# Keeping V of all batches in SBUF, and a first key projection by contraction halves, in a fused attention and mixture-of-experts kernel

## The reference

```python
x = x + tanh(g_xattn) * xattn(layernorm(x), ctx)      # 4 x 512 x 256, 16 heads of 16
x = x + tanh(g_ffn) * ffn(layernorm(x))

def xattn(x, mem):                     # 512 queries and 512 keys in each of 4 batches
    k, v = split(mem @ W_kv); q = x @ W_q
    return softmax(q @ k.T / 4) @ v @ W_proj + b_proj

def ffn(x):                            # 2048 tokens, 8 experts, the best 2 of each token, and a shared one
    logits = x @ gate_w.T; weights = softmax(top2(logits))
    return shared(x) + sum over the 2 chosen e of weight * (silu(x @ wg[e].T) * (x @ wu[e].T)) @ w_down[e].T
```

## Time and profile before

| | |
|---|---|
| median of 3 runs | 529.23 us |
| profiled execution, its own time | 531.15 us |
| its span (first to last instruction) | 529.4 us |
| TensorE busy | 503.8 us, 95% of the span |
| VectorE, ScalarE, GpSimd busy | 56%, 51%, 32% |
| moved by DMA | 58.60 MB |

### The profile page before, as it was taken

The page is one execution under the profiler, slowest core; times in us unless marked ns, Lnnn a source line. Parts: engine busy times, 40 slices in busy tenths (PEclk is TensorE's granted clock), DMA queues, the critical chain, the costliest instruction groups (busy, mean ns, idle before and its releaser), DMA issues.

```text
span 529.4 us, 8545 instructions
## 1 busy us (share of the span) xinstructions
PE 503.8 (95%) x2972; PEld 316.4 (60%) x2972; DVE 295.5 (56%) x537; ACT 271.9 (51%) x436; POOL 171.8 (32%) x193
## 2 busy tenths in 40 slices
PE   8989899999999999999989989999999999999992
PEld 6645423333333333334456456589999999999991
DVE  3665777887887888883565993233333333333321
ACT  1756267777777777775564301205444444444430
POOL 4400166672211111111000003004655666665542
PEclk9999989999999999999999998999999999999997
DMA  7999419987773666300013002112444333344332
GB/s 253 305 284 255 185 36 254 250 200 216 195 178 92 169 170 169 81 1 23 0 41 120 1 0 80 41 41 71 65 66 69 63 61 61 62 66 66 63 45 30
DMA packets 44882, 58.60 MB, mean 111 GB/s; under 512 B 6352, under 2 KB 36688, under 8 KB 44336
## 3 DMA queue, kind: packets, MB, share of 16 engines
q1 hardware_dynamic: 29536, 36.12, 25.7%
q0 software_dynamic: 7488, 10.23, 11.9%
q10 hardware_dynamic: 7824, 11.81, 6.7%
HBM read 37.89 MB, written 20.05 MB: 109 GB/s over the span
## 4 chain that ended last, share of the span: by engine, by line
PE 76%; DVE 9%; DMA 8%; issue 2%; ACT 2%; SPq 2%; POOLq 1%; POOL 0%; DVEq 0%
PE ps L1095 59%; PE ps L1181 12%; DMA out<-unit_region 5%; DMA x_sb<-in_x 2%; PE ps L1189 2%; PE ps L1467 1%; DVE neg_max L819 1%; DMA unit_region<-qk_parts 1%; DVE ctx_region L1022 1%; DVE unit_region L1014 1%; SPq L344 1%; DVE unit_region L931 1%; ACT ctx_region L675 1%; PE ps L1298 1%; DVE stats L776 1%
## 5 line engine op out<-in xcount | busy, mean ns | idle before, releaser
L819 DVE TENSOR_REDUCE neg_max<-ps 128x2 f32<-128x1024 f32 x128 | 151.2, 1219 | 43.3 <-PE ps L1095 42.9
L675 ACT ACTIVATE ctx_region<-ps 128x512 f32<-128x512 f32 x256 | 139.9, 595 | 58.8 <-PE ps L1095 58.6
L1095 PE MATMUL ps<-unit_region 96*128 96x512 bf16 (+1 forms) x512 | 134.1, 383 | 4.5 <-DMA unit_region<-qk_parts 2.1
L1095 PE MATMUL ps<-unit_region,ctx_region 128*128 128x128 f32 (+1 forms) x968 | 115.4, 277 | 2.5 <-DVE x_sb L938 2.5
L1095 PEld LDWEIGHTS ps<-unit_region,ctx_region 128*128 128x128 f32 (+1 forms) x968 | 111.7, 190 | 3.7 <-DVE x_sb L938 3.4
L1095 PEld LDWEIGHTS ps<-unit_region 96*128 96x128 bf16 (+1 forms) x512 | 48.4, 99 | 98.3 <-ACT ctx_region L675 58.9
L562 POOL DMA_INDIRECT out<-unit_region x39 | 61.8, 1585 | 55.7 <-DMA out<-unit_region 50.8
L535 POOL DMA_INDIRECT unit_region<-x_rows,unit_region x39 | 38.6, 989 | 123.0 <-DVE unit_region L1049 81.0
L1095 PE MATMUL ps<-dn_region,unit_region 128*128 (+1 forms) x330 | 78.2, 379 | 0.0
L741 ACT COPY ctx_region<-up_region 128x1536 f32 x39 | 57.3, 1472 | 35.0 <-PE ps L1095 34.9
L1181 PE MATMUL ps<-ctx_region,unit_region 128*32 128x512 f32 x512 | 68.7, 609 | 2.2 <-ACT ctx_region L675 0.7
(11 more groups left out here) (151 smaller groups left out, 407.6 us busy)
## 6 DMA issues: line engine op xcount, KB each, us to landing
up_region<-in_w_upT ACTq DMA_DIRECT2D x9, 768.0 KB, 4.3
qk_parts<-up_region SPq DMA_DIRECT2D x32, 192.0 KB, 3.2
unit_region<-qk_parts SPq DMA_DIRECT2D x32, 192.0 KB, 4.5
v_rows<-dn_region SPq DMA_DIRECT2D x4, 1024.0 KB, 5.9
unit_region<-qk_parts SPq DMA_DIRECT2D x32, 128.0 KB, 4.4
unit_region<-v_rows SPq DMA_DIRECT2D x16, 256.0 KB, 5.5
dn_region<-in_w_downT ACTq DMA_DIRECT2D x9, 384.0 KB, 5.5
ctx_region<-in_ctxT SPq DMA_DIRECT2D x4, 512.0 KB, 10.9
```

Of the source, the lines that this page charges most:

```text
L675: nc.scalar.activation(probs[:, k % 8, :], bank(4 + k % 2), ACT.Exp).then_inc(exp_done, 1)
L819: nc.vector.tensor_reduce(neg_max[:, s, 2 * p:2 * p + 2], bank(2 * (p % 2), 2), AX.X, ALU.max, negate=True).then_inc(max_done, 1)
L1095: return nc.tensor.matmul(o_, w, m, start=start, stop=stop)
```

## The change

V gets a home in SBUF for each batch: batches 0, 1 and 2 in `dn_region` (batch 2 where `resid` was), batch 3 in `unit_region`. `v_rows`, `send_v` and `load_v` go, with 4 stores of 1024 KB and 16 loads of 256 KB. The ones are set in three memsets at the old place, and a fourth once the last `low_part` is through. The w_down loads of ScalarE are moved to slots in which their place in `dn_region` is free. The first key projection waits for each half of the contraction by itself (`first_k`), and for that w_kv's K half and ctx of batch 0 are loaded in two halves each; w_kv's V half goes to ScalarE's queue and x of batch 0 to SP's, behind them. TensorE's loop over slots is written out. Its wait for `whole_sb` is moved from ahead of slot 0 to step 3 of it.

```diff
+PARTS_SENT = {1: (0, 1), 5: (2,), 9: (3,)}
+UP_AT = (1, 2, 3, 5, 6, 7, 9, 10, 11)
+DOWN_AT = (13, 14, 15, 5, 6, 9, 10, 11, 1)
-    v_rows = nc.dram_tensor("v_rows", (B, P, TB, H * VW), F32, kind="Internal").ap()
...
+        V_AT = (2 * DC * T, 2 * DC * T + v_words, 0)
+        def v_home(b):
+            home = (dn_region[:, V_AT[b]:V_AT[b] + v_words] if b < len(V_AT) else unit_region[:, 4 * HG * T:unit_words])
+            return home.rearrange("p (k h w) -> p k h w", k=TB, h=H)
...
-            sp.dma_start(wkv_sb[:, :, 0:D], w_kv_rows[:, :, 0:D]).then_inc(wk_in, 16)
-            load_ctx(0)
-            sp.dma_start(wkv_sb[:, :, D:2 * D], w_kv_rows[:, :, D:2 * D]).then_inc(wv_in, 16)
+            for d in range(DC):
+                sp.dma_start(wkv_sb[:, d, 0:D], w_kv_rows[:, d, 0:D]).then_inc(k_half[d], 16)
+                sp.dma_start(ctx_sb[:, d, 0:T], ctxT[d * P:(d + 1) * P, 0:T]).then_inc(k_half[d], 16)
+            sp.dma_start(x_sb[:, 0:TB, :], x_dram[:, 0:TB, :]).then_inc(x_in[0], 16)
...
             send_k(0)
-            send_v(0)
             send_q(0)
...
-            nc.gpsimd.memset(v_sb[:, :, :, :, HD:VW], 1.0).then_inc(v_ones, 1)
-            pool.wait_ge(v_ones, 1)
+            for n, b in enumerate((0, 1, 3)):
+                nc.gpsimd.memset(v_home(b)[:, :, :, HD:VW], 1.0).then_inc(v_ones, 1)
+                pool.wait_ge(v_ones, n + 1)
...
+            pool.wait_ge(low_done, len(QK_ORDER) // 2)
+            nc.gpsimd.memset(v_home(2)[:, :, :, HD:VW], 1.0).then_inc(v_ones, 1)
...
-            act.dma_start(x_sb[:, 0:TB, :], x_dram[:, 0:TB, :]).then_inc(x_in[0], 16)
+            act.dma_start(wkv_sb[:, :, D:2 * D], ...[:, :, D:2 * D]).then_inc(wv_in, 16)
...
-                if b >= 2:
-                    act.wait_ge(v_out[b - 2], 16)
+                if b == 2:
+                    act.wait_ge(low_done, len(QK_ORDER) // 2)
...
+            for u in range(1, UNITS):
+                if u in PARTS_SENT: (waits for k_out and q_out of these batches, as before)
+                if u in UP_AT:
+                    load_up(UP_AT.index(u))
+                if u in DOWN_AT:
+                    if u > NG:
+                        act.wait_ge(pv_done, (u - 1) // NG * NG * TB)
+                    load_down(DOWN_AT.index(u))
                 exp_slot(u, u % NG, more_max=u + 1 < UNITS)
...
-                    last = nc.tensor.matmul(bank(6)[...], v_unit[:, s, kt, h * VW:(h + 1) * VW],
+                    last = nc.tensor.matmul(bank(6)[...], v_home(u // NG)[:, kt, u % NG * HG + h, :],
...
-                pe.wait_ge(v_in[s], 16 * (bu + r // NG + 1))
+                pe.wait_ge(v_done, u // NG + 1)
...
                         if first:
                             pe.wait_ge(nmT_sb, 1)
+                            pe.wait_ge(whole_sb, len(WHOLE_ORDER))
...
+            def first_k():
+                for d in range(DC):
+                    pe.wait_ge(k_half[d], 16 * 2)
+                    for c in range(DC):
+                        last = mm(bank(K_BANK + c), wkv_sb[:, d, c * P:(c + 1) * P], ctx_sb[:, d, 0:T], d == 0, d == DC - 1)
+                last.then_inc(k_ps, 1)
...
             pe.wait_ge(ones_rows, 1)
+            pe.wait_ge(v_ones, B)
             pe.wait_ge(rowsT_sb, B)
-            pe.wait_ge(whole_sb, len(WHOLE_ORDER))
             slot(0, 0, 0, first=True)
-            with pe.Fori(0, B - 1) as b:
-                for r in range(1, NG + 1):
-                    slot(b * NG + r, b, r)
+            for u in range(1, UNITS - 3):
+                slot(u, (u - 1) // NG, (u - 1) % NG + 1)
```

More of the change, by code:

```diff
@@ L244, in build @@
         ctx_in = [sem(f"ctx_in{b}") for b in range(B)]
-        wk_in, wv_in, wq_in = sem("wk_in"), sem("wv_in"), sem("wq_in")
+        k_half = [sem(f"k_half{d}") for d in range(DC)]
+        wv_in, wq_in = sem("wv_in"), sem("wq_in")
         gates_in = sem("gates_in")
@@ L367, in send_k @@
                 send_parts(1, b, k_out[b])
[L369 to L372, removed]
             def send_q(b):
@@ L391, in _ @@
                 load_rows(0, g, 0, q_unit, Q_RUNS)
[L392 to L395, removed]
             for g in range(2, NG):
@@ L568, in _ @@
         def _(act):
-            act.dma_start(x_sb[:, 0:TB, :], x_dram[:, 0:TB, :]).then_inc(x_in[0], 16)
+            act.dma_start(wkv_sb[:, :, D:2 * D], w_kv.rearrange("(c p) n -> p c n", p=P)[:, :, D:2 * D]).then_inc(wv_in, 16)
             act.dma_start(wq_sb[:, :, :], w_q.rearrange("(c p) n -> p c n", p=P)).then_inc(wq_in, 16)
@@ L613, in copy_v @@
                     act.wait_ge(v_ones, 1)
-                if b >= 2:
-                    act.wait_ge(v_out[b - 2], 16)
-                nc.scalar.copy(v_sb[:, b % 2, :, :, 0:HD],
+                if b == 2:
+                    act.wait_ge(low_done, len(QK_ORDER) // 2)
+                nc.scalar.copy(v_home(b)[:, :, :, 0:HD],
                                bank(V_BANK, 2).rearrange("p a (k h w) -> p (a k) h w", k=2, h=H)).then_inc(v_done, 1)
@@ L650, in _, with load_up, load_down @@
             whole_q(3)
[L652 to L657, removed]
+            def load_up(e):
+                act.dma_start(w_up[:, e, :, :], w_upT[e, :, :].rearrange("(c p) f -> p c f", p=P)).then_inc(w_ffn_in, 16)
+            def load_down(e):
+                act.dma_start(w_dn[:, e, :, :], w_downT[e, :, :].rearrange("(c p) n -> p c n", p=P)).then_inc(w_ffn_in, 16)
             def copy_max(u):
@@ L681, in _ @@
             exp_slot(0, 0, first=True)
-            for b in range(B):
-                act.wait_ge(v_out[b], 16)
-            for b in range(B - 1):
-                for late in ((0, 1), (2,), (3,))[b]:
-                    act.wait_ge(k_out[late], 16 * QK_OUTS)
-                    act.wait_ge(q_out[late], 16 * QK_OUTS)
-                for r in range(1, NG + 1):
-                    if r < NG:
-                        load_expert(b * 3 + r - 1)
-                    exp_slot(b * NG + r, r % NG)
-            for u in range(UNITS - 3, UNITS):
+            for u in range(1, UNITS):
+                if u in PARTS_SENT:
+                    for b in PARTS_SENT[u]:
+                        act.wait_ge(k_out[b], 16 * QK_OUTS)
+                        act.wait_ge(q_out[b], 16 * QK_OUTS)
+                if u in UP_AT:
[4 more added lines that the diff above has]
+                    load_down(DOWN_AT.index(u))
                 exp_slot(u, u % NG, more_max=u + 1 < UNITS)
@@ L1180, in pv @@
                 for h in range(HG):
-                    last = nc.tensor.matmul(bank(6)[h * VW:(h + 1) * VW, :], v_unit[:, s, kt, h * VW:(h + 1) * VW],
+                    last = nc.tensor.matmul(bank(6)[h * VW:(h + 1) * VW, :], v_home(u // NG)[:, kt, u % NG * HG + h, :],
                                             probs[:, (kt * HG + h) % 8, :], start=kt == 0, stop=kt == TB - 1,
@@ L1235, in _ @@
             TURN_MAX, TURN_OUT = 3, 9
-            for b in range(2):
-                project_k(b, 0)
-                project_k(b, 1)
+            def first_k():
[4 more added lines that the diff above has]
+                last.then_inc(k_ps, 1)
+            for b in range(2):
+                if b == 0:
+                    first_k()
+                else:
+                    project_k(b, 0)
+                    project_k(b, 1)
                 project_v(b, (0, 1))
```

18 lines of the change are left out of this document (3 added, 15 removed).

## The result

The changed kernel takes 532.30 us in the median of 9 runs (530.39 to 533.98); the kernel before took 529.55 us beside it (9 runs, 528.89 to 530.81). The ratio is 1.0047, with a 95% interval of 1.0030 to 1.0064: it is slower by 2.75 us. The prediction was 527.9 us in a range of 526.4 to 530.6, with a chance of 0.18 for slower. The profiled execution of the changed kernel took 532.3 us, with a span of 530.5 us.

A forecast was written before the change was run, and what follows sets the result against it. TensorE, busy 95% of the span, was taken to bound the kernel, with a chain of waits in the first 82 us; +1.0 - 0.6 - 1.5 - 0.2 = -1.3 us from 529.23 gave 527.9 us, range 526.4 to 530.6.

The forecast's parts named there:

- the term of +1.0 us: x of batch 0 behind 768 KB lands at 10.2 (bounds 8.8 to 12.2), delaying `first_pair(0, 0)` by 1.0 us (0 to +3.0).
- the clock in the projections: TensorE's clock falling in idleness ahead of `turn_xn(0)` or `first_pair(0, 0)`; left out of the sum, kept as a rival.
- the landing less 9.2: Delay of the chain to `first_pair(0, 0)` equals the landing time of x of batch 0 minus 9.2 us.
- The first key projection, up to 0.43 us sooner: With half the data needed, the projection begins up to 0.43 us sooner; the gain ends at `turn_xn(0)`.
- The slower rival: Clock falls in the projections, first at `turn_xn(0)` after 1.7 us idle (1.3 on the chain); both places 530.9 us; chance 0.15.
- the second place: TensorE's wait ahead of `first_pair(0, 0)`, where a fall of the clock would cost 1.7 us.
- The moved wait and the clock at slot 0, -0.6 and -1.5: At slot 0, less waiting for `whole_sb` gains 0.6 us; the clock staying at 2.4 GHz from 66 to 70 gains 1.5.
- the signs of being wrong: x landing before 9 or after 12, the clock falling at another place, or the slots getting shorter.
- V's traffic at nothing: In the attention slots, taking 8 MB of V's transfers out of the DMA rings gains nothing by itself.
- the loop, -0.2 to -0.3: Writing out TensorE's loop over slots saves 0.2 us at two round ends (bounds 0 and -0.3).
- the w_down loads at nothing: Loads ahead of slots 13 to 15 on ScalarE's queue cost 0, at most +1.4 us; rival +0.2, 529.4 us, chance 0.05 with the rest.
- their cover of 2 us: Memsets start at 14.0 and `copy_v(0)` needs the first at 17.1; without cover 0.9 us goes on the path.

The follow-up runs named there:

- ctx_halves: Changed kernel with K projected in one piece and w_kv's K half loaded whole, ctx of batch 0 still in two halves; 530.86 us, ratio 1.0035 to the kernel before.
- swap_whole: Changed kernel with whole loads and K projected in one piece, x of batch 0 still behind 768 KB on SP's queue; 528.48 us, ratio 0.9992 to before.
- old_start: Changed kernel with the loads and first key projection of the kernel before, rest of the change kept; 527.78 us, ratio 0.9975 to before.
- filler: Changed kernel with 14 transposes of nothing on TensorE ahead of `turn_xn(0)`; 532.34 us, ratio 1.0060 to the kernel before.
- new_start: Kernel before with only the changed kernel's start (halves, w_kv's V half on ScalarE's queue, x on SP's); 534.18 us, ratio 1.0087 to before.
- whole_ahead: Changed kernel with the wait for `whole_sb` back ahead of slot 0; 533.81 us, ratio 1.0078 to the kernel before.
- wait_only: Kernel before with only the wait for `whole_sb` moved to step 3 of slot 0; 528.52 us, ratio 0.9973 to before.

## Why the prediction was wrong

**The step that failed is the landing of x of batch 0, the term of +1.0 us; the runs give +2.8.** A second failed with it, the clock in the projections, which the sum put at nothing and which cost 1.5. The rule of the first, the landing less 9.2, was good: 12.0 gives +2.8 for the changed kernel, and 11.8 gives +2.6 for ctx_halves, where `apply_rows(1)` came 2.4 us later. Its size was off. I had costed x by the bytes ahead of it, between two landings of whole loads. swap_whole shows that this gives 9.7. The halves, which I had only counted as bytes, brought it to 12.0, the upper part of my own bounds.

**The first key projection, up to 0.43 us sooner**: it started at 7.61 instead of 7.70, but its second half landed at 9.5, where the whole ctx of batch 0 had landed at 7.6. It then took 3.93 us instead of 3.67, and V's products started 0.17 us later than before, at 11.38. The halves gained nothing over the kernel before, and they are what separates the changed kernel from swap_whole, 3.8 us; x's place on the queue costs at most the 0.7 us between swap_whole and old_start, whose intervals overlap.

**The slower rival came true at its first place.** `turn_xn(0)` found TensorE idle for 2.58 us, not 1.7, and the clock fell; the transposes and V's second half took 0.7 and 1.0 us longer. The rival's price for this was 1.3; the profiles above give 1.5. I had set against it that 2 us of idleness at 34 to 36 let the clock stand, which was one stretch of one profile. At the second place, ahead of `first_pair(0, 0)`, it stood this time too. Over the profiles it fell behind idle times of 2.6, 2.6, 3.0, 3.2 and 4.5 us and stood behind 1.2, 1.2, 1.4 and (filler) 2.4 us.

**Not foreseen: `high_k(0)` waits too.** ScalarE takes the standard deviation of batch 0, which needs x, ahead of it; it ran at 14.07, though K was ready at 11.5. In the kernel before it ran at 11.4. Behind the same x, VectorE's residue and the parts of K of batch 0 came later. It isn't on the chain here, and no run separates it.

**The moved wait and the clock at slot 0, -0.6 and -1.5.** The wait was right: 0.7 to 0.8 us in the profiles. The clock's term was right in size for the one profile it was read from (1.1 us up to the first product with V and some 0.5 us behind it), but it was taken off a median that need not have had that fall, and new_start and whole_ahead keep the wait and show no fall there. Both steps together are 1.4 us (0.3 to 2.6) by wait_only's ratio and 0.5 by its medians, where the sum had 2.1. How often the clock falls can be read from the mean granted clock over the span of the 111 runs of the kernel before beside the experiments: 0.995 in 17 runs, which average 527.2 us; 0.991 or 0.992 in 67, 529.1 us; 0.988 or 0.989 in 24, 530.9 us. The profiled execution, with 531.15 us, is like the third group, the median like the second. It tells the number of falls and not their place: the profile of before has two stretches of low clock ahead of 500 us, at 66 to 70 and at 316 to 324, the changed kernel's has one at 16 to 20 and one at 320 to 324, and which of the two the median run of before lacks is not known. For the changed kernel 4 of 9 runs have 0.991 (530.9 us) and 5 have 0.988 or less (533.1 us). So part of the 2.75 us is that it goes one level down more often, and 1.8 us is the distance at the level of 0.991.

**The sum with the measured terms**: +2.8 (x) + 1.5 (clock in the projections) - 1.4 (wait and clock at slot 0) - 0.3 (loop) = +2.6 us, against 2.75 measured. The third term is known only to about 1 us, so the agreement is partly luck. Of the signs of being wrong that the prediction named, one came (the clock fell at another place), and one stood at its edge (x after 12).

**Right as they stood**: V's traffic at nothing (old_start against wait_only); the loop, -0.2 to -0.3 with V's moves in it; the w_down loads at nothing, for over the last slots, with the new loads in them, the changed kernel takes as long as the one before (270.28 - 215.53 = 54.75 us, and 271.42 - 216.67 = 54.75, between two products with V). What a round end costs is less sure than it looked: the changed kernel has no loop and still takes 12.32 us from slot 5 to 6. The memsets were covered in the changed kernel; in ctx_halves two of them lie on the chain, at 15.7 to 17.7 us, so their cover of 2 us goes when x is late.

**Open**: by what means an additional load at the head of SP's queue delays those behind it, why x's landing varies by up to 2.2 us between kernels with the same loads, why filler's median shows none of the 1.5 us of its profile, and what lets the clock fall at 268 us in some profiles.

## What to carry to other kernels

Before a load is split so that its first half comes sooner, look at who stands behind it on the queue and when that one is needed: here two more issues at the head of a queue cost a load behind them 2.3 us, for nothing gained in front. Price a load's landing by loads of the same number and size ahead of it, not by bytes alone. And when a profile shows a fallen clock, compare its own time with the median before counting on getting it back, and look for other places where it falls: a fall that is gone in one place came at another in four of the profiles here.

## What was unexpected of the hardware

- With two DRAM-to-DRAM transfers of 1 KB near the head of SP's queue, it was nearly still for 2 us (0.02 MB from 6 to 8 us against 0.43), with 512 KB issued behind them; those landed 2.0 us later, for an issue 1.5 us later.
- A load of 512 KB cut in two made the packets of its queue slower: 126 instead of 230 of them in 2 us, for the same share of the engines' time.
- Taking 0.14 MB of loads in very small pieces off ScalarE's queue brought a load on SP's queue 1.1 us forward in one profile; taking 256 KB in pieces of 1 KB off it brought nothing.
- With the same loads ahead of it, x landed anywhere from 12.0 to 14.2 us in four profiles.
- Run times of one kernel stand in levels 1.8 us apart, which go with the mean granted clock over the span (0.995, 0.991, 0.988; 108 of 111 runs).
- A fall of the clock in the projections cost 1.5 us on the chain (10.04 us instead of 8.52 from x's landing to `apply_rows(1)`, three profiles against four).
